# Patch embedding in a ViT layer: float32 products replaced by three float16 products, with the split of the image on ACT and DVE

## The reference

```python
hidden = jnp.einsum('npd,hd->nph', patches, W_lin) + b_lin
h = jnp.concatenate([cls, hidden], axis=1)
h = h + attention(layernorm(h))
h = h + experts(layernorm(h))
```

## Time and profile before

| | value |
|---|---|
| median of three runs | 2130.58 us |
| profiled execution, its own time | 2126.83 us |
| its span, first to last instruction | 2124.9 us |
| phase A in the span | from the first embedding at 28.7 us to about 1,160 us |
| busy over the whole span | PE 90%, DVE 62%, ACT 43% |
| TensorE clock granted over the span | 0.984 of full speed |

### The profile page before, as it was taken

The page is one execution under the profiler, slowest core; times in us unless marked ns, Lnnn a source line. Parts: engine busy times, 40 slices in busy tenths (PEclk is TensorE's granted clock), DMA queues, the critical chain, the costliest instruction groups (busy, mean ns, idle before and its releaser), DMA issues. The chain is left out here.

```text
span 2124.9 us, 48134 instructions
## 1 busy us (share of the span) xinstructions
PE 1922.6 (90%) x17848; PEld 1351.2 (64%) x17848; DVE 1320.9 (62%) x3554; ACT 908.2 (43%) x1878; POOL 42.2 (2%) x63
## 2 busy tenths in 40 slices
PE   3999989899899898998998699999999999999998
PEld 3777767677677776776776355555555555555556
DVE  3444444444344444444444488788888888888888
ACT  2555545455455555555555233333333333333332
POOL 0000000000000000000000000000000000000000
PEclk9999999999999999999999799999999999999999
DMA  4011111111111111111110000000000000000000
GB/s 146 16 45 44 48 43 45 46 44 45 46 45 44 46 44 46 45 45 46 44 44 10 32 16 30 17 21 23 15 30 15 22 22 15 30 15 30 16 21 13
DMA packets 31517, 74.83 MB, mean 35 GB/s; under 512 B 3435, under 2 KB 16366, under 8 KB 31214
## 3 DMA queue, kind: packets, MB, share of 16 engines
q1 hardware_dynamic: 31310, 72.10, 10.8%
HBM read 52.73 MB, written 19.37 MB: 34 GB/s over the span
## 5 line engine op out<-in xcount | busy, mean ns | idle before, releaser
L571 ACT ACTIVATE prob<-ps_sc 99x792 f32<-99x792 f32 x384 | 317.5, 827 | 256.0 <-PE ps_sc L413 256.0
L357 PE MATMUL ps_hid<-lin_f,xin 128*99 128x192 f32 x1536 | 289.9, 333 | 65.7 <-DVE v L684 36.1
L905 PE MATMUL ps_h<-yT_hi,w_hi 96*128 96x512 f16 (+1 forms) x900 | 342.8, 381 | 0.0
L907 PE MATMUL ps_h<-yT_lo,w_hi 96*128 96x512 f16 (+1 forms) x900 | 341.3, 379 | 0.0
L908 PE MATMUL ps_h<-yT_hi,w_lo 96*128 96x512 f16 (+1 forms) x900 | 340.9, 379 | 0.0
L357 PEld LDWEIGHTS ps_hid<-lin_f,xin 128*99 128x99 f32 x1536 | 240.3, 169 | 77.0 <-issue 47.2
L979 ACT ACTIVATE in_hi<-inner 128x512 f16<-128x512 f32 (+1 forms) x225 | 140.3, 624 | 338.3 <-DVE inner L1098 338.3
L923 PE MATMUL ps_y<-w_hi,in_hi 128*128 128x192 f16 (+1 forms) x900 | 222.4, 247 | 40.6 <-DVE acc L1122 29.0
L971 ACT ACTIVATE act<-ps_h 128x512 f32<-128x512 f32 (+1 forms) x225 | 132.3, 588 | 278.6 <-PE ps_h L908 277.9
L1122 DVE SCALAR_TENSOR_TENSOR acc<-ps_y,comb,acc 128x192 f32<-128x192 f32 (+1 forms) x700 | 242.3, 407 | 0.0
L1098 DVE SCALAR_TENSOR_TENSOR inner<-ps_h,act 128x512 f32<-128x512 f32 (+1 forms) x225 | 152.7, 679 | 130.0 <-ACT act L971 119.8
(11 more groups left out here) (112 smaller groups left out, 3050.1 us busy)
## 6 DMA issues: line engine op xcount, KB each, us to landing
xin<-xp SPq DMA_DIRECT2D x64, 594.0 KB, 3.9
hidden_dram<-h SPq DMA_DIRECT2D x64, 147.0 KB
hin<-hidden_dram SPq DMA_DIRECT2D x24, 384.0 KB, 3.0
out<-acc SPq DMA_DIRECT2D x24, 384.0 KB, 2.3
w_f<-w SPq DMA_DIRECT2D x1, 1728.0 KB, 11.5
hidden_dram<-h SPq DMA_DIRECT2D x64, 0.8 KB
w_f<-w SPq DMA_DIRECT2D x1, 864.0 KB, 13.0
lin_f<-w_lin SPq DMA_DIRECT2D x1, 576.0 KB
```

Of the source, the lines that this page charges most:

```text
L357: last = pe.matmul(hid[:, t, :], xin[q][:, k, t * TR:(t + 1) * TR], lin_f[:, k, :], start=(k == 0), stop=(k == PCHUNKS - 1))
L571: act.activation(prob[quad][:, places].rearrange("p h m s -> p h (m s)"), ps_sc[0:TR, places, 0:2 * SLOTS], ACT.Exp, scale=D ** -0.5 / (SQ ...
L905: pe.matmul(bank[:, 0:N], w13_hi[:, k, e, w, :], yT_hi[p][:, k, 0:N], start=(k == 0), stop=False)
L907: pe.matmul(bank[:, 0:N], w13_hi[:, k, e, w, :], yT_lo[p][:, k, 0:N], start=False, stop=False)
```

## The change

The embedding goes from 12 float32 matmuls per image to 36 float16 ones. ACT makes the leading half of the image, scaled by 64 (`x_hi`), and DVE the remainder (`x_lo`), each in two pieces of three chunks, in step k, ahead of `embed(k, 0)`. `lin_f` moves from the constants to the second place of the weights and gets its pair in the setup. `xin` goes from four buffers to two. The bias is now added by an operation that also divides by the scale. 16 steps are written out ahead of the loop.

```diff
-            weights = [(qkv_f, qkv_hi, qkv_lo, w_qkv),
+            weights = [(qkv_f, qkv_hi, qkv_lo, w_qkv), (lin_f, lin_hi, lin_lo, w_lin),
...
-            others = [(lin_f, w_lin), (id32, ident), (biascls, bias_cls), (gbias, gate_bias), (bef4, before4), (bef8, before8)]
-            xin = [sb(f"xin{p}", [128, PCHUNKS, SLOTS]) for p in range(4)]
+            others = [(id32, ident), (biascls, bias_cls), (gbias, gate_bias), (bef4, before4), (bef8, before8)]
+            xin = [sb(f"xin{p}", [128, PCHUNKS, SLOTS]) for p in range(2)]
+            x_hi = [sb(f"x_hi{p}", [128, PCHUNKS, SLOTS], F16) for p in range(2)]
+            x_lo = [sb(f"x_lo{p}", [128, PCHUNKS, SLOTS], F16) for p in range(2)]
...
-            first = 1
+            first = 2
...
-                if reached(n.times(1, -3)):
-                    sp.wait_ge(hid_done, n.times(1, -3))
-                sp.dma_start(xin[q][:], xp[n.times(1)]).then_inc(x_in[q], 16)
+                if reached(n.times(2, -2)):
+                    sp.wait_ge(xlo_done, n.times(2, -2))
+                sp.dma_start(xin[p][:], xp[n.times(1)]).then_inc(x_in[p], 16)
...
-                    pe.wait_ge(x_in[q], n.quarters(16, 16))
+                    pe.wait_ge(xlo_done, n.times(2, 2))
...
-                    last = pe.matmul(hid[:, t, :], xin[q][:, k, t * TR:(t + 1) * TR], lin_f[:, k, :],
-                                     start=(k == 0), stop=(k == PCHUNKS - 1))
+                    pe.matmul(hid[:, t, :], x_hi[p][:, k, s], lin_hi[:, k, :], start=(k == 0), stop=False)
+                    pe.matmul(hid[:, t, :], x_hi[p][:, k, s], lin_lo[:, k, :], start=False, stop=False)
+                    last = pe.matmul(hid[:, t, :], x_lo[p][:, k, s], lin_hi[:, k, :],
+                                     start=False, stop=(k == PCHUNKS - 1))
...
+            def split_x(n, part):
+                p, own = n.mod(2), slice(3 * part, 3 * part + 3)
+                if part == 0:
+                    act.wait_ge(x_in[p], n.halves(16, 16))
+                    if reached(n.times(1, -1)):
+                        act.wait_ge(hid_done, n.times(1, -1))
+                act.activation(x_hi[p][:, own, :], xin[p][:, own, :], ACT.Copy, scale=SX).then_inc(xhi_done, 1)
...
                     exponent(n3, 0, 1)
+                if k.active():
+                    split_x(k, 0)
...
                     square(n2, 1)
+                if k.active():
+                    split_x(k, 1)
+                if n2.active():
                     qk_rstds(n2, 1)
...
+            def split_x(n, part):
+                p, own = n.mod(2), slice(3 * part, 3 * part + 3)
+                dve.wait_ge(xhi_done, n.times(2, part + 1))
+                dve.scalar_tensor_tensor(out=x_lo[p][:, own, :], in0=xin[p][:, own, :], scalar=SX,
+                                         in1=x_hi[p][:, own, :], op0=ALU.mult,
+                                         op1=ALU.subtract).then_inc(xlo_done, 1)
...
-                dve.tensor_tensor(h[q][:], hid, biascls[:], ALU.add).then_inc(h_done, 1)
+                dve.scalar_tensor_tensor(out=h[q][:], in0=hid, scalar=1.0 / SS, in1=biascls[:],
+                                         op0=ALU.mult, op1=ALU.add).then_inc(h_done, 1)
...
                     norm_hidden(n1)
+                if k.active():
+                    split_x(k, 0)
                 if n2.active():
                     qk_variance(n2, 1)
+                if k.active():
+                    split_x(k, 1)
+                if n2.active():
                     qk_normalise(n2, 1)
```

More of the change, by code:

```diff
@@ L94, in halves @@
         return self.i * (self.unroll // 2 * per) + (self.c // 2 * per + plus)
-    def quarters(self, per, plus=0):
-        return self.i * (self.unroll // 4 * per) + (self.c // 4 * per + plus)
     def mod(self, m):
@@ L120, in split_pair @@
                 return sb(name + "_hi", shape, F16), sb(name + "_lo", shape, F16)
+            lin_hi, lin_lo = split_pair("lin", [128, PCHUNKS, C])
             qkv_hi, qkv_lo = split_pair("qkv", [KC, 2, 3 * C])
@@ L239, in phase_a @@
 def phase_a(nc, xp, hidden_dram, sem, bufs):
-    (lin_f, qkv_hi, qkv_lo, proj_hi, proj_lo, id32, biascls, eps, eps_qk, xin,
+    (lin_hi, lin_lo, x_hi, x_lo, qkv_hi, qkv_lo, proj_hi, proj_lo, id32, biascls, eps, eps_qk, xin,
      h, stats, meanvar, h_rstd, h_lnvar, xnorm, xT_hi, xT_lo, qk_sq, qk_var, qk_lnvar, qk_rstd,
@@ L248, in phase_a @@
         bufs[n] for n in (
-            "lin_f qkv_hi qkv_lo proj_hi proj_lo id32 biascls eps eps_qk xin "
+            "lin_hi lin_lo x_hi x_lo qkv_hi qkv_lo proj_hi proj_lo id32 biascls eps eps_qk xin "
             "h stats meanvar h_rstd h_lnvar xnorm xT_hi xT_lo qk_sq qk_var qk_lnvar qk_rstd "
@@ L270, in phase_a @@
         o_quad = ps_o[:, 0:SLOTS]
-        x_in = [sem(f"x_in{p}") for p in range(4)]
+        x_in = [sem(f"x_in{p}") for p in range(2)]
         h2_out = [sem(f"h2_out{p}") for p in range(2)]
@@ L281, in phase_a @@
         qkT_out, v_set, oT_out, onThi_done = sem("qkT_out"), sem("v_set"), sem("oT_out"), sem("onThi_done")
+        xhi_done, xlo_done = sem("xhi_done"), sem("xlo_done")
         h_done, stats_done, mv_done = sem("h_done"), sem("stats_done"), sem("mv_done")
@@ L308, in load @@
             def load(n):
-                q = n.mod(4)
-                if reached(n.times(1, -3)):
-                    sp.wait_ge(hid_done, n.times(1, -3))
-                sp.dma_start(xin[q][:], xp[n.times(1)]).then_inc(x_in[q], 16)
+                p = n.mod(2)
+                if reached(n.times(2, -2)):
+                    sp.wait_ge(xlo_done, n.times(2, -2))
+                sp.dma_start(xin[p][:], xp[n.times(1)]).then_inc(x_in[p], 16)
             def store(n):
@@ L356, in embed @@
                     t, k = j // PCHUNKS, j % PCHUNKS
-                    last = pe.matmul(hid[:, t, :], xin[q][:, k, t * TR:(t + 1) * TR], lin_f[:, k, :],
-                                     start=(k == 0), stop=(k == PCHUNKS - 1))
+                    s = slice(t * TR, (t + 1) * TR)
+                    pe.matmul(hid[:, t, :], x_hi[p][:, k, s], lin_hi[:, k, :], start=(k == 0), stop=False)
+                    pe.matmul(hid[:, t, :], x_hi[p][:, k, s], lin_lo[:, k, :], start=False, stop=False)
+                    last = pe.matmul(hid[:, t, :], x_lo[p][:, k, s], lin_hi[:, k, :],
+                                     start=False, stop=(k == PCHUNKS - 1))
                 if part == 2:
```

## The result

The changed kernel takes 2265.18 us (median of 4 runs, 2263.81 to 2268.3), against 2131.0 for the kernel before in the same runs: a ratio of 1.0627, with an interval from 1.0606 to 1.0648. It is slower, as forecast, but by 134 us where 56.7 were forecast, and above the range of 2147 to 2212.

| stretch | before | after | difference |
|---|---|---|---|
| start to the first `v_copy` on DVE | 47.50 | 54.79 | +7.3 |
| first to last `v_copy` (63 intervals, phase A) | 1111.04 | 1229.75 | +118.7 |
| the rest (end of phase A, phase B) | 966.4 | 977.4 | +11.0 |
| span | 2124.9 | 2261.9 | +137.0 |

The account below looks back on a forecast made before the run. The prediction took a chain through ACT and DVE, ahead of PE in each step, as the bound. Steps +57.3, setup +4.1 and loop -4.7 us sum to +56.7; against the median it forecast 2187 us, range 2147 to 2212.

Parts of the forecast that it names:

- The chain: Path over ACT and DVE to `residual`, which PE awaits: 1.25 us later, less 0.31 saved, +0.94 us per step.
- First pieces: Split pieces on the path, ACT's ahead of `oT_copy` and DVE's behind `xnorm`: +0.57 and +0.68 us per step.
- second pieces: Split pieces behind `square` on ACT and behind `qk_variance` on DVE: they fit into idle time and add nothing.
- part 0: Embedding part at the end of the step on PE: its 0.31 us count in full, parts 1 and 2 nothing.
- Rival 3: PE's longer wait lowers TensorE's clock in every step: 207 us more, about 2394 us; chance 0.03.
- The loop: Ends of phase A's loop passes: 6 passes left of 7, one stop of 4.7 us goes, -4.7 us.
- The setup: Start of the kernel: 1.9 us for loading `lin_f` earlier and about 2.2 for the bare first split, together +4.1.

Follow-up runs that it names:

- e9: Changed kernel with ACT's pieces of the split alone; DVE makes the remainder for the first two images only: 2171.16 us, ratio 1.0204.
- e10: Changed kernel with DVE's pieces of the split alone; ACT makes the leading half for the first two images only: 2208.62 us, ratio 1.0383.
- e2: Changed kernel with the split made for the first two images only, on both engines, and used for all: 2127.21 us, ratio 0.9995.
- e1_fill: Changed kernel with 20 extra float16 matmuls, read by nobody, on PE ahead of its wait for `residual`: 2208.83 us, ratio 1.038.
- e7: Kernel before the change with 16 steps written out ahead of the loop in place of 8: 2119.84 us, ratio 0.9963.
- e5: Changed kernel with 60 semaphore increments more on DVE, once, at the start of phase B: 2252.26 us, ratio 1.0578.
- e6: e4 with 60 semaphore increments more on DVE, once, at the start of phase B: 2108.26 us, ratio 0.9906.
- e4: Changed kernel with the split moved to the end of the step and the embedding one step later: 2128.74 us, ratio 1.0002.

## Why the prediction was wrong

The 137 us of the spans: about 57 for the chain (61 x 0.93), 44 for the clock in the long steps, 17 for dearer stops at pass ends (5 x 8.8 against 6 x 4.5; 13.3 of it came back with the filler), 7 in the setup, 11 in phase B, and 1 that is not divided further. Of the 80 us beyond the forecast, the clock in the long steps makes 44, the stops 22, phase B 11 and the setup 3.

- **The chain: right**, in every term. First pieces +0.57 and +0.68, second pieces hidden, part 0 alone counting: e9, e10 and e2 measured each by itself, and +0.93 per step stands in e1_fill.
- **The clock: the step that failed first.** Rival 3 had the mechanism and got 0.03. The argument was that the new wait of 1.8 us is shorter than the stops at pass ends and that 0.55 us show nothing. Neither says anything of 1.8 us that recur in every step: one is a rare long wait, the other a frequent short one, and the new one was outside both. The honest reading was that the trace didn't show it, so the price is open. The prediction's own sign of being wrong, a clock below 0.95 in phase A, came true with 0.92. The size of rival 3 was wrong the other way: I took 3.4 us lost in each step; it was 1.4 us in 31 of 57. A drop lasts some 3 us, which loses about 1.6 us of work at full speed; that slack ahead of `xT_lo` and `kT` swallows the rest is argued, not shown. The rule that I cited from the Trainium skill (TensorE: Matmul & The Clock Gate, A second HAM failure mode), stated there for a kernel that cycles through PSUM banks, is borne out here for a wait on DVE: the clock swings between its levels with 1.84 us of idling per step, and doesn't with 0.58.
- **The loop: wrong sign.** I priced a stop at the 4.7 us of the rows before, as if that belonged to a stop. With the clock behind it, it is 4.5 to 8.8 us depending on the kernel (e7 5.1, e1_fill 6.1, after 8.8), and in e7 one fewer was worth 1.7. By the estimate above the stop itself is some 2.8 us in both kernels: the one that went saved 3, and the clock behind the other five cost 20 more than before, so that with the long steps about 64 of the 137 us are the clock. The stop itself is not the same everywhere: e2 has 8.7 with no long wait in its steps, and at its clock of 0.84 in these intervals 4.1 of them go to the clock; the other 4.6 were not separated from the place and length of the code.
- **Phase B: no term at all.** I took unedited code for unchanged time. Its instructions moved, and DVE's loop lost up to 3.3 us at the end of a pass. The Trainium skill (Runtime: NRT & Kernel Launch, Instruction fetch mechanics) says that a taken branch whose target isn't among the pages held forces a fetch before execution goes on; e5 and e6 agree in that 60 instructions of shift end the stop of 3.3 us, but no trace here shows the fetch itself.
- **The setup: +4.1 forecast, +7.3 measured**: `w_hi` starts at 15.08 us (13.68 before), 1.4 of the 1.9 allowed; but in e7, which has the setup of the kernel before, it starts at 15.41, so single executions scatter by as much. The bare first split takes 2.2 us as forecast: its load lands at 29.93, and the first embedding starts at 32.20 (28.75 before, +3.45). The other 3.9 us come behind it, where PE's first steps run at a lower clock, 0.57 in this window (1.00 in the same window before):

```profile
39.00:47.00 8.00, 5.37 (x33) 5.17 (x34) 2.61 (x5) 1.55 (x4) 0.00 (x0) 0.57 0.24 76
```

## What to carry to other kernels

When an edit lengthens a wait of PE that recurs in every step, look at the granted clock in windows of 1 us, not at its mean, and try filler matmuls in the wait: they cost nothing if PE idles there, and tell the clock's share from the chain's. Put work that has a step's time to spare where nobody on the chain stands behind it; here the same instructions at the end of the step cost nothing. And before believing a result of a per cent, look for waits on issue in stages that the edit doesn't touch, and write the loop out or shift it once to see what the code's place does.

## What the runs showed of the hardware

- TensorE's clock fell to its 1.2 GHz level for about 3 us behind a wait of 1.84 us per step of 18 us, in 31 of 57 steps; 1.14 to 1.25 us did it in 7 to 10 of 57 steps, 0.58 us in none. 20 matmuls in the wait, 1.32 us of PE, ended it.
- 60 increments at a place that runs once made the kernel some 10 us faster, and e4's version 20.5, by shifting a loop of DVE, whose stops of 3.3 us went.
- A stop at the end of a pass of phase A cost 2.8 to 3.0 us where the clock stayed at 1.00 (two intervals of the kernel before, 20.2 and 20.4 us against 17.38), and 8.8 on average where it stood at 0.78 (the changed kernel). Without a loop, 64 steps of written-out code ran with no stop at all, in 16.87 us each once the pipeline was full.
